# A two-stage cross-attention block on one core: where a head's weighted chunks stand in their tick, and which queue takes the large transfers

## What is computed

```
x = x + attention0(x, ctx)[0]                     # layer 0
xq, y = layer_norm(x, gq, bq), layer_norm(ctx, gkv, bkv)
q = (xq @ Wq) split in 16 heads; k, v = (y @ Wkv) split in 16 heads
o = softmax(q @ k.T * SCALE) @ v
x = x + o @ Wproj + bproj
x = x + gelu(layer_norm(x, gm, bm) @ W1 + b1) @ W2 + b2
```

## Time and profile before

| | |
|---|---|
| median of 3 runs | 1885.4 us (1879.6 to 1895.0) |
| the profiled execution's own time | 1889.9 us |
| its span, first to last instruction | 1888.1 us |
| mean granted TensorE clock in it | 0.972 |
| TensorE, ScalarE, VectorE, GpSimd busy | 93, 62, 58, 50% of the span |
| DMA moved | 354.7 MB, 188 GB/s |
| w_r<-w_scratch, issued by ScalarE | 214 of 512 KB, 5.1 us from issue to landing |
| q_st<-negmax_t, issued by SP | 576 of 0.5 KB |
| out<-xres, issued by SP | 7 of 1024 KB, 8.6 and 9.4 us; 4 of 256 KB, 2.0 us |

### The profile page before, as it was taken

One profiled execution on the slowest core, in us unless ns is written; L12 is line 12 of the kernel. 1 busy time (PEld: TensorE's weight loads), 2 busy tenths in 40 slices (PEclk: granted clock), 3 DMA queues, 4 the chain that ended last, 5 costly groups with the idle time before them and its releaser, 6 DMA issues.

```text
span 1888.1 us, 23894 instructions
## 1 busy us (share of the span) xinstructions
PE 1750.5 (93%) x7488; PEld 1339.1 (71%) x7488; DVE 1094.3 (58%) x1860; ACT 1166.9 (62%) x1935; POOL 935.6 (50%) x778
## 2 busy tenths in 40 slices
PE   6899999887898899999999999999999999999898
PEld 5677777655566677767667767777776677677687
DVE  4566655565676565756655655656566666654322
ACT  3677774677777666756756576667566565765231
POOL 0455422476764464546544554655455455546331
PEclk8999999999999999999999999999999999999999
DMA  6689945787545664675466455646654774557262
GB/s 231 220 286 294 310 173 177 270 276 237 183 125 176 162 185 132 189 201 165 141 201 182 143 157 172 197 126 186 205 160 138 211 187 143 157 168 243 81 237 89
DMA packets 156382, 354.69 MB, mean 188 GB/s; under 512 B 28512, under 2 KB 47072, under 8 KB 155360
## 3 DMA queue, kind: packets, MB, share of 16 engines
q1 hardware_dynamic: 125440, 240.95, 41.8%
q10 hardware_dynamic: 30816, 112.21, 19.1%
HBM read 251.51 MB, written 82.08 MB: 177 GB/s over the span
## 4 chain that ended last, share of the span: by engine, by line
PE 69%; ACT 8%; DVE 6%; DMA 6%; issue 5%; POOL 3%; SPq 3%; DVEq 0%; ACTq 0%; POOLq 0%
PE ps_d L862 46%; PE ps_o L911 11%; PE ps_t L894 5%; PE ps_s L879 5%; DMA q_st<-negmax_t 3%; SPq L637 2%; DVE negmax L1147 1%; ACT ps_d L927 1%; DMA k_st<-k_scratch 1%; PE ps_d L792 1%; DVE rs_t L1126 1%; ACT p_hi L1006 1%; ACT ps_t L1013 1%; ACT L1006 1%; DVE stats L1104 1%
## 5 line engine op out<-in xcount | busy, mean ns | idle before, releaser
L1257 POOL TENSOR_TENSOR p_lo<-p_full,p_hi 128x512 fp32r<-128x512 f32 x288 | 371.5, 1290 | 633.9 <-ACT p_full L1013 631.2
L1006 ACT ACTIVATE p_hi<-ps_t 128x512 fp32r<-128x512 f32 x576 | 345.2, 599 | 417.0 <-PE ps_t L894 416.1
L1147 DVE TENSOR_REDUCE negmax<-ps_s 128x1 fp32r<-128x512 f32 x576 | 389.9, 680 | 187.5 <-PE ps_s L879 187.2
L862 PE MATMUL ps_d<-hT,w_r 128*128 128x512 f32 x1536 | 432.3, 398 | 3.5 <-DVE hT L1052 1.8
L862 PE MATMUL ps_d<-w_r,g_s 128*128 128x512 f32 x1536 | 399.7, 398 | 5.5 <-DMA w_r<-w_scratch 5.5
L862 PEld LDWEIGHTS ps_d<-hT,w_r 128*128 128x128 f32 x1536 | 293.0, 191 | 81.7 <-DVE hT L1052 3.0
L862 PEld LDWEIGHTS ps_d<-w_r,g_s 128*128 128x128 f32 x1536 | 294.6, 192 | 77.2 <-issue 8.7
L1160 DVE TENSOR_TENSOR p_lo<-ps_t,p_hi 128x512 fp32r<-128x512 f32 x288 | 198.7, 690 | 231.4 <-ACT ps_t L1013 229.8
L911 PE MATMUL ps_o<-p_hi,v_s 128*65 128x512 f32 x576 | 236.6, 411 | 45.9 <-ACT o_raw L1029 40.9
L894 PE MATMUL ps_t<-q_st,k_st 97*128 97x512 f32 x576 | 235.8, 409 | 32.3 <-DMA q_st<-negmax_t 32.2
L879 PE MATMUL ps_s<-k_st,q_st 96*128 96x512 f32 x576 | 236.8, 411 | 11.3 <-DVE negmax L1147 9.6
(11 more groups left out here) (99 smaller groups left out, 2185.1 us busy)
## 6 DMA issues: line engine op xcount, KB each, us to landing
w_r<-w_scratch ACTq DMA_DIRECT2D x214, 512.0 KB, 5.1
w_r<-w_scratch SPq DMA_DIRECT2D x42, 512.0 KB, 4.7
v_scratch<-v_out SPq DMA_DIRECT2D x36, 520.0 KB, 3.9
...
```

The source lines that it names most:

```text
L862: ins = nc.tensor.matmul(bank(u), lhs[a], rhs[b], start=(i == 0 and m == 0), stop=(i == 3 and m == 2))
L1006: act.activation(p_hi[:, c], ps_t[:, c % 2], ACT.Exp, scale=SCALE)
L1147: dve.tensor_reduce(negmax[:, h % 2, c:c + 1], ps_s[:, c % 2], AX.X, ALU.max, negate=True).then_inc(s_maxed, 1)
L1257: pool.tensor_tensor(p_lo[:, c], p_full[:, (by_gpsimd(s) - 1) % 2], p_hi[:, c].bitcast(F32), ALU.subtract).then_inc(p_pool_split, 1)
```

## The change

1. On TensorE, a head's chunk 3 (`weighted % TC == TC - 1`) now stands first in its tick, ahead of `s`; chunks 1 and 2 stay where they were; chunk 0 stands last, behind fill 2. On ScalarE the copy to `o_raw` follows the two exps of the tick at once, and the evacuations of position 1 and the Gelu halves (`g_s`) come behind it.
2. From `SHARED_FROM` on (tick 89, two ticks into pass 1) ScalarE issues the stores of q, the values, the residual, the outputs of passes 1 to 7, the stages, the W2 pieces and `wo`, all behind the tick's computing instructions. SP keeps rows, stacks, placed heads, late weights and the last pass's output.
3. The residual goes in four pieces of 256 KB, one per tick from three ticks ahead of the next pass (pass 1: all four at one tick), and so does the output of passes 1 to 7, each piece two ticks after its last matmul. A W2 piece is stored four ticks behind its split in place of two.

The moved functions (`load_values`, `store`, `load_stage`, `load_piece`, `store_piece`) are unchanged but for a parameter that says which queue issues; they are left out here.

```diff
     for n in range(1, NP):
-        res.append((PLAN.base[n + 1] - (40 if n == 1 else 0), n))
-        if n < NP - 1:
-            outs.append((PLAN.end("y2", n, 15) + 1, (n, -1)))
-        else:
-            outs += [(PLAN.end("y2", n, 12 + t) + 1, (n, t)) for t in range(TC)]
+        res += [(PLAN.base[n + 1] + (t - 3 if n > 1 else -40), (n, t)) for t in range(TC)]
+        outs += [(PLAN.end("y2", n, 12 + t) + (2 if n < NP - 1 else 1), (n, t)) for t in range(TC)]
...
+SHARED_FROM = PLAN.base[1] + 2
...
+        queue.dma_start(xres[n % 2][:, t], rows(x, n - 1)[:, t]).then_inc(res_loaded[n % 2], 16)
+
+    def store_out(queue, n, t):
+        queue.wait_ge(evacuated, ready("y2", n, 12 + t))
+        queue.dma_start(rows(out, n - 1)[:, t], xres[n % 2][:, t]).then_inc(out_stored[n % 2], 16)
...
         for tick in range(TICKS):
             for h in ROWS.get(tick, []):
                 load_row(h)
-            for u in STORES.get(tick, []):
-                store(*u)
+            early = tick < SHARED_FROM
+            for u in STORES.get(tick, []) if early else ():
+                store(sp, *u)
             for h in HEADS.get(tick, []):
                 load_stack(h)
             for h in PLACES.get(tick, []):
                 place_head(h)
-            for n, g in VALUES.get(tick, []):
-                load_values(n, g)
-            for n in RES_LOADS.get(tick, []):
-                load_residual(n)
+            for n, g in VALUES.get(tick, []) if early else ():
+                load_values(sp, n, g)
...
         for tick in range(TICKS):
+            weighted = PLAN.pv_at.get(tick)
+            if weighted is not None and weighted % TC == TC - 1:
+                values(weighted)
             s = PLAN.s_at.get(tick)
...
             fill(tick, 1)
-            s = PLAN.pv_at.get(tick)
...
+            if weighted is not None and weighted % TC in (1, 2):
+                values(weighted)
             fill(tick, 2)
+            if weighted is not None and weighted % TC == 0:
+                values(weighted)
...
                 act.activation(whole, ps_t[:, c % 2], ACT.Exp, scale=SCALE).then_inc(p_exp, 1)
+            s = PLAN.pv_at.get(tick)
+            if s is not None and s % TC == TC - 1:
+                h = s // TC
+                act.wait_ge(pv_done, s + 1)
+                if h >= 2:
+                    act.wait_ge(o_placed[(h - 2) % G], ((h - 2) // G + 1) * (16 * PLACE_DMAS))
+                act.activation(o_raw[0:VW, h % 2], ps_o[0:VW], ACT.Identity).then_inc(o_moved, 1)
             for u in EVACUATED.get((tick, True), []):
                 evacuate(*u)
...
+            late = tick >= SHARED_FROM
+            for u in STORES.get(tick, []) if late else ():
+                store(act, *u)
             for kind, j in W_LOADS.get(tick, []):
                 load_weight(kind, j)
+            for n, g in VALUES.get(tick, []) if late else ():
+                load_values(act, n, g)
+            for n, t in OUT_STORES.get(tick, []):
+                if n < NP - 1:
+                    store_out(act, n, t)
+            for n, t in RES_LOADS.get(tick, []):
+                load_residual(act, n, t)
+            for kind, b in STAGE_LOADS.get(tick, []) if late else ():
+                load_stage(act, kind, b)
```

More of the change, by code:

```diff
@@ L619, in xattn_program, with load_values, store @@
     block = block_cm.__enter__()
+    def load_values(queue, n, g):
+        i = n * G + g
+        if i >= 2:
+            queue.wait_ge(pv_done, (i - 1) * G * TC)
+        if g == 0:
+            for c in range(TC):
+                j = V_NO["v", n, c]
+                queue.wait_ge(v_stored[j % 2], 16 * (j // 2 + 1))
+        queue.dma_start(v_s[:, i % 2].rearrange("p c h e -> p c (h e)").bitcast(F32),
+                     vd[n, g]).then_inc(v_loaded[i % 2], 16)
+    def store(queue, kind, n, i):
+        queue.wait_ge(evacuated, ready(kind, n, i))
+        if kind == "v":
+            j = V_NO[kind, n, i]
+            queue.dma_start(vd[n, :, :, i].rearrange("g p e -> p g e"),
+                         v_out[:, j % 2].rearrange("p (g h) e -> p g (h e)", g=G).bitcast(F32))\
+                .then_inc(v_stored[j % 2], 16)
+        else:
+            j = KQ_NO[kind, n, i]
+            queue.dma_start((kd if kind == "k" else qd)[n, i * P:i * P + P],
+                         kq_out[:, j % 2].bitcast(F32)).then_inc(kq_stored[j % 2], 16)
@@ L765, in _ @@
             for n, t in OUT_STORES.get(tick, []):
-                store_out(n, t)
-            for kind, b in STAGE_LOADS.get(tick, []):
-                load_stage(kind, b)
+                if n == NP - 1:
+                    store_out(sp, n, t)
+            for kind, b in STAGE_LOADS.get(tick, []) if early else ():
+                load_stage(sp, kind, b)
             if tick == PRE:
-                load_stage("y", 1)
+                load_stage(sp, "y", 1)
             for name, at in WHOLE_LOAD.items():
@@ L773, in _ @@
                     load_whole(name)
[L774 removed]
+            for i in range(PIECES // 2):
                 if tick == piece_tick(i) - 3:
[L776 removed]
+                    load_piece(sp, i)
                 if tick == piece_tick(i) + 2:
[L778 to L781 removed]
+                    store_piece(sp, i)
         last = NP - 1
[L783 to L784 removed]
+        sp.wait_ge(out_stored[last % 2], 16 * TC * (last // 2))
+        sp.wait_ge(out_stored[(last - 1) % 2], 16 * TC * (last // 2))
     @block.tensor
@@ L868, in fill, with values @@
                 part(kind, n, c, i)
+        def values(s):
+            h, c = divmod(s, TC)
+            group = h // G
+            if c == 0:
+                if h:
+                    pe.wait_ge(o_moved, h)
+                if h % G == 0:
+                    pe.wait_ge(v_loaded[group % 2], 16 * (group // 2 + 1))
+            if c in POOL_CHUNKS:
+                pe.wait_ge(p_pool_split, by_gpsimd(s))
+            else:
+                pe.wait_ge(p_split, by_vector(s))
+            for m, src in enumerate((p_hi, p_lo)):
+                ins = nc.tensor.matmul(ps_o[0:VW], v_s[:, group % 2, c, h % G], src[:, c],
+                                       start=(c == 0 and m == 0), stop=(c == TC - 1 and m == 1))
+            ins.then_inc(pv_done, 1)
         pe.wait_ge(ident_loaded, 16)
         for tick in range(TICKS):
+            weighted = PLAN.pv_at.get(tick)
+            if weighted is not None and weighted % TC == TC - 1:
+                values(weighted)
             s = PLAN.s_at.get(tick)
@@ L1287, in _ @@
                 if t == 0:
[L1288 removed]
+                    pool.wait_ge(res_loaded[n % 2], 16 * TC * ((n + 1) // 2))
                     pool.wait_ge(bias_added, TC if n > 1 else 1)
```

136 lines of the change are left out of this document (43 added, 93 removed).

## The result

| | before | after |
|---|---|---|
| median | 1889.1 us (4 runs, 1879.6 to 1895.0) | 1835.1 us (4 runs, 1833.9 to 1837.3) |
| ratio | | 0.9711, interval 0.9669 to 0.9753 |
| profiled execution, its span | 1889.9, 1888.1 us | 1835.2, 1833.4 us |
| mean granted clock | 0.972 | 0.982 |

A forecast was written before the change was run, and what follows sets the result against it. TensorE, busy 93% of the span, bounds the kernel, so only its idle time or clock can pay. 31.6 + 14 + 18 + 5 - 5 - 11 = 53 us off 1885.4 gives 1833 us; own range 1812 to 1855, 80% range 1811 to 1872.

The forecast's parts named there:

- Rows, 31.6 us: PE's waits for the small row DMAs (30.1 us) and `k_st` (1.5) all vanish once rows leave the large transfers' queue.
- Pass 1 gives back 11: In pass 1, half of 21 us gained on rows and clock returns as waits for POOL and VectorE: 11 us lost.
- Order, 18 us: PE's waits for `o_raw` and POOL's late chunk 0 shrink with last weighted chunk first, first one last: 18 us gained.
- Clock, 14 + 5 us: Half-clock PE work after stalls shrinks: 14 us behind row stalls (bounds 0 and 15.5), 5 behind `o_raw` stalls (0 and 15).
- ScalarE's issues, 5 us: 142 DMAs moved to ScalarE cost 5 us, 29 stores at 0.15 us; bounds 0 and 121.
- Pass 3: Sign in the profile after: pass 3 takes some 167 us instead of 175.7.
- The first one, rows no sooner: Rival: DMA engines are full, so only SP's own lateness on the rows goes; 1847 us, chance 0.17.
- the place of 814.70: Pass 3: PE's `ps_t` matmul stood 3.84 us until the row landed; the forecast had no such wait left.
- The second rival: Rival: the last chunk, now ahead of its tick, waits on PE for VectorE's `p_lo`; 1870 us, chance 0.09.
- The third: Rival: ScalarE is held by its transfers, stretched issues delaying exps that PE needs; 1912 us, chance 0.10.

The follow-up runs named there:

- the queues alone: Kernel after the change, with the weighted chunks and the o_raw copy back in the order of before, transfers of after kept: 1857.0 us, ratio 0.9838.
- quarters on SP: Kernel after the change, with its pieces, ticks and order, but SP issues all large transfers again: 1848.2 us, ratio 0.9786.
- 510 more issues: Kernel after the change, plus one 512-byte DMA issued by ScalarE at the end of every tick of passes 1 to 8: 1842.2 us, ratio 0.9742.
- the whole-transfer kernel of ScalarE's queue: Kernel after the change, but residual and output of passes 1 to 7 go whole at the ticks of before, on ScalarE's queue: 1835.8 us, ratio 0.9730.

## Why the prediction was right

Total: 53 us were forecast and 54 measured (1889.1 - 1835.1; the median of before was 1885.4 when there were three runs). The mechanisms held. Two terms were off by some 10 us each and cancelled, so that the total is right to 1 us is in part luck.

- **Rows, 31.6 us.** Measured 22.0. In passes 3 to 8 the stalls fell by 15.6 of 17.5; in passes 1 and 2 by 6.4 of 14.1. What failed there is "I take all of these away": SP stays 3.4 us late in pass 1 with small transfers alone, 2.0 of it in two issues that stretched.
- **Pass 1 gives back 11.** Measured about 1: in passes 1 and 2 `p_lo` waits rose by 4.4 us and `negmax` waits fell by 3.4. Of what I let return, 7.7 us had never been won. The net of pass 1, 21 - 11 = 10 us of rows and clock, stands beside 10.8 measured; that is the right number from two wrong ones.
- **Order, 18 us.** Measured 13.5. In the late passes it was right term by term (12.9 of 13.3: 2.88 to 2.16 for 2.2, 1.46 to 0.31 for 0.25, the third to nothing). In passes 1 and 2 the waits fell by 0.6, not by 5.1: the two large ones are 5.6 and 3.0 us, and the six small ones, nearly all of which I let go, are seven that hold 3.9.
- **Clock, 14 + 5 us.** 21 measured. Behind the row stalls the slow stretches fell by 27.2 us, which is 14 at most; behind the `o_raw` stalls by 17.0, which is 8 at most for the 5 forecast (the bound of 15 is half of 32.3, so 16). That the smaller `o_raw` stalls are the reason of the 8 is not shown: the queues alone have a slow stretch in three of six passes too, with the stalls at 2.9 us.
- **ScalarE's issues, 5 us.** At 0.014 us each, 142 cost 2 us.
- **Pass 3** took 167.7 us for the 167 forecast.

**The rivals.** The first one, rows no sooner, had the right account of the late passes and the wrong price. At the place of 814.70 the gain was SP's lateness, and landing gave 0.9 us; quarters on the shared queue reach pass 3 of 166.6 us. But lateness was enough to remove nearly the whole stall, so that its 13 us stood at 15.6, and pass 1 did gain by the queue: its profile is 159.3 us with quarters on SP and 153.8 after, and the row stalls of passes 1 and 2 are 12.2 and 7.7. (The other kernels with a queue for the rows have pass 1 at 154.7 to 159.0, so the size of that gain is uncertain.) The Trainium skill, DMA: Bandwidth & Descriptors, "Issuing engines are not separate DMA queues", says that spreading issues saves only issue time: passes 3 to 8 of the kernel with quarters on SP agree (1002.4 us against 999.5), its whole time (1848.2 against 1835.1, the intervals of the ratios just part) does not. Its section "Queues, rings and completion order" says that a DMA engine goes round the queues that have work: the row behind 1 MB of its own queue, up to 9.5 us, against at most 5.2 beside the same 1 MB of the other queue, agrees. The second rival shows as 1.6 us of waits for VectorE's `p_lo`, all in pass 1. The third does not show: 510 more issues cost 7 us.

**Open**: what of the 13 us that only both halves together give is more than the waits named; what the W2 pieces stored later do for pass 1; which stalls are followed by a slow stretch; and why SP's issues stretch in pass 1. A busy q10 alone does not do it: in the whole-transfer kernel of ScalarE's queue SP's stack issues at 792 us took 0.51 to 0.69 us with q10 at 87%.
